# One chunk pipeline of a macaron block: one-hots at slot 1, z in slot 1 and silu in slot 3, and GpSimd's second product with C in slot 2

## The reference, cut to what matters

```
x = x + 0.5 * ffn(layernorm(x))            # f1
x = x + attn(layernorm(x))                 # p
x = x + 0.5 * ffn(layernorm(x))            # f2

ffn:  idx = argmax(softmax(x @ Wg + bg))                  # one of 8 experts per token
      out = gelu(x @ W1[idx] + b1[idx]) @ W2[idx] + b2[idx]
attn: xn = rmsnorm(x) * w;  x_path, z = split(xn @ Win.T)  # 256 channels each
      x_path = silu(causal conv of 4 taps(x_path) + conv_b)
      dt_x, B, C = split(x_path @ Wx.T)                    # 128, 16, 16
      dt = softplus(dt_x @ Wdt.T + dt_b)
      h = exp(dt * A) * h + (dt * x_path) * B              # along the tokens, 16 states per channel
      y = sum(h * C) + D * x_path
      out = (y * silu(z)) @ Wo.T + x
```

## Time and profile before

| | before |
|---|---|
| median of 3 runs | 1440.38 us (1437.05 to 1445.34) |
| the profiled execution, its own time | 1439.62 us |
| its span | 1437.8 us |
| TensorE busy | 1166.5 us (81%) |
| VectorE busy | 1061.8 us (74%) |
| GpSimd busy | 1066.9 us (74%) |
| ScalarE busy | 872.5 us (61%) |
| granted clock of TensorE, mean | 0.886 of 2.4 GHz |

### The profile page before, as it was taken

The page is one execution under the profiler, slowest core; times in us unless marked ns, Lnnn a source line. Parts: engine busy times, 40 slices in busy tenths (PEclk is TensorE's granted clock), DMA queues, the critical chain, the costliest instruction groups (busy, mean ns, idle before and its releaser), DMA issues.

```text
span 1437.8 us, 16300 instructions
## 1 busy us (share of the span) xinstructions
PE 1166.5 (81%) x5188; PEld 572.8 (40%) x5188; DVE 1061.8 (74%) x1713; ACT 872.5 (61%) x1171; POOL 1066.9 (74%) x900
## 2 busy tenths in 40 slices
PE   2678585879899988889888989888888887866777
PEld 1234232424444434344444444343444443423345
DVE  2021688888888797888888788978888888988910
ACT  0333746577667577676766675766767676574532
POOL 1023789888888797978888887979788888997600
PEclk9877697989899999899998999999999998878688
DMA  3002332323224051323233230503232323232000
GB/s 87 0 0 96 121 124 88 127 88 112 96 81 141 25 190 33 136 79 125 96 118 104 96 112 27 196 25 136 79 124 89 118 98 112 103 126 88 1 8 15
DMA packets 60406, 130.02 MB, mean 90 GB/s; under 512 B 7745, under 2 KB 26865, under 8 KB 52129
## 3 DMA queue, kind: packets, MB, share of 16 engines
q1 hardware_dynamic: 60320, 128.98, 26.1%
HBM read 106.94 MB, written 22.02 MB: 90 GB/s over the span
## 4 chain that ended last, share of the span: by engine, by line
PE 48%; DVE 24%; ACT 14%; POOL 6%; issue 6%; SPq 1%; DVEq 0%; ACTq 0%; DMA 0%; POOLq 0%
PE PY L479 12%; PE PH L464 11%; DVE dA L765 10%; PE G L453 9%; PE Y L491 6%; ACT hs L616 4%; DVE hb L769 4%; ACT dA L638 3%; PE PH L463 3%; DVE hb L763 3%; ACT hs L603 2%; POOL hb L943 2%; PE G L519 2%; ACT L616 2%; DVE stat L744 1%
## 5 line engine op out<-in xcount | busy, mean ns | idle before, releaser
L943 POOL TENSOR_TENSOR hb<-dtx_rep,bs 128x1024 f32<-128x1024 f32 x256 | 598.4, 2357 | 0.0
L765 DVE TENSOR_TENSOR_SCAN dA<-dA,hb 128x512 f32<-128x512 f32 x352 | 429.6, 1221 | 63.7 <-ACT dA L638 56.5
L638 ACT ACTIVATE dA<-dt_rep,A 128x512 f32<-128x512 f32 x512 | 341.0, 689 | 160.3 <-DVE hb L769 102.7
L464 PE MATMUL PH<-xnT,W 128*128 128x512 f32 x512 | 325.1, 720 | 0.0
L603 ACT COPY hs<-PH 128x512 f32<-128x512 f32 x256 | 149.2, 583 | 288.7 <-PE PH L464 288.5
L479 PE MATMUL PY<-W,hs 128*128 128x128 f32 x2048 | 294.7, 290 | 0.0
L479 PEld LDWEIGHTS PY<-W,hs 128*128 128x128 f32 x2048 | 259.8, 197 | 69.6 <-issue 60.0
L951 POOL TENSOR_TENSOR hb<-hb,cs 128x1024 f32<-128x1024 f32 x80 | 188.4, 2355 | 119.4 <-DVE hb L763 119.4
L769 DVE TENSOR_TENSOR hb<-dA,cs 128x512 f32<-128x512 f32 x352 | 243.5, 692 | 24.8 <-DVE dA L765 0.5
L763 DVE TENSOR_TENSOR_SCAN hb<-dA,hb 128x512 f32<-128x512 f32 x160 | 186.4, 1207 | 60.0 <-ACT dA L638 56.7
L491 PE MATMUL Y<-hb,Sel 128*32 128x512 f32 x1024 | 162.0, 707 | 30.9 <-POOL hb L951 23.7
(11 more groups left out here) (85 smaller groups left out, 1172.6 us busy)
## 6 DMA issues: line engine op xcount, KB each, us to landing
dtx_rep<-dtx_rows SPq DMA_DIRECT2D x32, 1024.0 KB, 6.4
dt_rep<-dt_rows SPq DMA_DIRECT2D x32, 1024.0 KB, 7.7
bs<-bc_rows SPq DMA_DIRECT2D x64, 256.0 KB, 3.6
cs<-bc_rows SPq DMA_DIRECT2D x64, 256.0 KB, 4.8
dtx_rows<-dtx SPq DMA_DIRECT2D x32, 256.0 KB, 2.5
dt_rows<-dt SPq DMA_DIRECT2D x32, 256.0 KB, 2.6
X<-in_x SPq DMA_DIRECT2D x16, 256.0 KB, 3.1
out<-X SPq DMA_DIRECT2D x16, 256.0 KB, 2.4
```

Source lines behind the costliest of these rows:

```text
L464: nc.tensor.matmul(PH[:, :], W1[:, e, :], xnT[:, w, :], start=False, stop=True).then_inc(ph_full, 1)
L638: nc.scalar.activation(dA[u % NA][:, :], dt_rep[:, h, g, :], ACT.Exp, scale=A[:, h, g, q:q + 1]).then_inc(decay, 1)
L765: nc.vector.tensor_tensor_scan(a, a, x_in_hb, 0.0, ALU.mult, ALU.add).then_inc(scan, 1)
L943: nc.gpsimd.tensor_tensor(hb[:, s % HR], dtx_rep[:, h, 2 * m:2 * m + 2, :], bs[:, q, None, :].broadcast_to([P, 2, CH]), ALU.mult).then_inc ...
```

## The change

Only the order of the work and one split between engines change.

- ln_f1 is transposed at the head of slot 0 (was slot 1), and ScalarE copies it to xnT between the two gelus of the iteration before (was behind slot 1).
- gate_f1 moves from slot 2 to the end of slot 0, its one-hot arithmetic on VectorE from ahead of slot 3 to ahead of slot 1. The transposes of the one-hots move from slot 5 to slot 6, behind the dt products, and their copy from ahead of slot 6 to ahead of slot 7.
- z0 and z1 move from slots 2 and 3 to slot 1. ScalarE's silu block moves from ahead of slot 4 to ahead of slot 3; the out product from slot 4 to slot 3, its add to behind slot 3, with the y add of f2 (was behind slot 2) ahead of it; bc, dt1 and dt0, their copies and softplus each one slot ahead.
- The statistics of f2 and GpSimd's root, norm, dt and dtx move one slot ahead. SyncE stores out and loads x in slot 5 (was 4), stores B and C in slot 5 (was 6) and the dt rows in slot 8 (was 9).
- GpSimd multiplies by C in slot 2, not in slot 3; VectorE does so in slot 3.
- A few units of the first and second products move within or by one slot.

```diff
-STAGES = [("ln_f1", 3, 0, 1, 0), ("gate_f1", 3, 1, 2, 1), ("z0", 1, 0, 2, 2), ("z1", 1, 1, 3, 1),
-          ("out", -1, 0, 4, 1), ("oh_f1", 3, 1, 5, 1), ("bc", 1, 0, 5, 0), ("dt1", 1, 1, 6, 0),
-          ("dt0", 1, 0, 6, 1), ("ln_f2", -1, 1, 9, 0), ("gate_f2", -1, 0, 10, 1), ("oh_f2", -1, 1, 12, 0),
+STAGES = [("ln_f1", 3, 0, 0, 0), ("gate_f1", 3, 1, 0, 2), ("z0", 1, 0, 1, 0), ("z1", 1, 1, 1, 2),
+          ("out", -1, 0, 3, 1), ("bc", 1, 0, 4, 1), ("dt1", 1, 1, 5, 0), ("dt0", 1, 0, 5, 1),
+          ("oh_f1", 3, 1, 6, 0), ("ln_f2", -1, 1, 9, 0), ("gate_f2", -1, 0, 10, 1), ("oh_f2", -1, 1, 12, 0),
           ("ln_p", 2, 0, 13, 0), ("x1", 2, 1, 14, 0), ("x0", 2, 0, 14, 1)]
-ACT_AT = {"ln_f1": 1.5, "silu": 4.0, "bc": 5.5, "dt1": 6.5, "dt0": 6.5, "soft": 7.0, "gelu_f2": 10.5,
-          "ln_f2": 9.5, "ln_p": 13.5, "taps": 14.0, "gelu_f1": 15.5}
-DVE_AT = {"gated1": 1.5, "y_f2": 2.5, "gate_f1": 3.0, "out": 4.5, "oh_f1": 6.0, "stats_f2": 5.0, "gated0": 9.5,
+ACT_AT = {"silu": 3.0, "bc": 4.5, "dt1": 5.5, "dt0": 5.5, "soft": 6.0, "gelu_f2": 10.5, "ln_f2": 9.5, "ln_p": 13.5,
+          "taps": 14.0, "gelu_f1": 15.5}
+DVE_AT = {"gate_f1": 1.0, "gated1": 1.5, "y_f2": 3.5, "out": 3.5, "stats_f2": 4.0, "oh_f1": 7.0, "gated0": 9.5,
           "y_f1": 10.0, "stats_p": 10.5, "gate_f2": 11.0, "stats_f1": 12.0, "oh_f2": 13.0, "tap01": 15.0, "tap2": 15.5}
-POOL_AT = {"root_f2": 6.5, "norm_f2": 7.0, "dt": 8.0, "dtx": 8.5, "root_p": 11.0, "norm_p": 12.0, "root_f1": 12.5,
+POOL_AT = {"root_f2": 5.5, "norm_f2": 6.0, "dt": 7.0, "dtx": 7.5, "root_p": 11.0, "norm_p": 12.0, "root_f1": 12.5,
            "norm_f1": 13.0}
-SP_AT = {"x_out": 4, "x_in": 4, "bc": 6, "b0": 8, "dt": 9, "b1": 10, "c0": 10, "b2": 12, "c1": 12, "b3": 14, "dtx1": 14,
+SP_AT = {"x_out": 5, "x_in": 5, "bc": 5, "b0": 8, "dt": 8, "b1": 10, "c0": 10, "b2": 12, "c1": 12, "b3": 14, "dtx1": 14,
          "c2": 14, "dt1": 15, "c3": 15}
-W1_AT = [[(8, 2, 8, 0, 3), (9, 2, 9, 0, 3), (10, 0, 10, 0, 3), (10, 2, 10, 3, 3),
+W1_AT = [[(8, 0, 8, 0, 3), (9, 0, 9, 0, 3), (10, 0, 10, 0, 3), (10, 2, 10, 3, 3),
...
-W2_AT = [[(s, 1, 2) for s in (5, 7, 7, 8, 8, 8, 9, 9)],
-         [(13, 1, -2), (14, 1, -2), (15, 1, -2), (15, 2, -2), (0, 1, -3), (0, 1, -3), (1, 1, -3), (1, 1, -3)]]
+W2_AT = [[(s, 1, 2) for s in (5, 6, 7, 7, 8, 8, 9, 9)],
+         [(13, 1, -2), (14, 1, -2), (15, 1, -2), (15, 2, -2), (0, 1, -3), (0, 1, -3), (1, 1, -3), (2, 1, -3)]]
...
-POOL_C = (1, 3, 5, 9, 14)
+POOL_C = (1, 2, 5, 9, 14)
...
                     if k == 0:
                         take_units(it, s, 3)
+                        if w == 0 and it.has(off + 1):
+                            copy_out(it.next(), "ln_f1", xnT[:, 0, :])
...
-                for w in range(2):
-                    if t == ACT_AT[f"ln_f{w + 1}"] and it.has(LN_OFF[w]):
-                        copy_out(it, f"ln_f{w + 1}", xnT[:, w, :])
+                if t == ACT_AT["ln_f2"] and it.has(-1):
+                    copy_out(it, "ln_f2", xnT[:, 1, :])
```

More of the change, by code:

```diff
@@ L172, in before, with next @@
         return Iteration(self.i0 - 1)
+    def next(self):
+        return Iteration(self.i0 + 1)
     def tiles(self, off, j=0, n=J):
```

## The result

The changed kernel takes 1375.68 us (median of 4 runs, 1373.46 to 1376.51) against 1440.31 (1437.05 to 1445.34): a ratio of 0.9546, 95% interval 0.9516 to 0.9576. The direction was right; the forecast of 1402 with its range down to 1383 was too slow by 26 us. The profiled execution has a span of 1374.2 us, 63.6 less than the 1437.8 of before.

The account below looks back on a forecast made before the run. VectorE's waits, partly behind TensorE's backlog, were taken as the bound. Eleven full iterations at 3.2 us (35), plus 8 for partial ones, 0 for fill and drain, less 5 for the clock, gave 38 off 1440.4: 1402, range 1383 to 1437.

Parts of the forecast that it names:

- What bounds it: Full iterations: VectorE idles 12.8 of 78.8 us, partly behind a TensorE backlog starting at its 2.50 us stall for bank 1.
- Slots 15 to 1: Iteration start: second gelu at 696.7, a 2.3 us wait for logits, slot 1 at 701.3, 1.4 us later than before.
- The out add: Slots 1 to 4: VectorE's add of the out product to X waits no more, 0.71 us won.
- Slots 4 to 10: TensorE runs without pause to 736.8; slot 10 starts at 737.5 instead of 740.61; 3.2 us taken per iteration.
- hidden, as said: GpSimd's moved work costs nothing, covered by its 2.5 us wait for the statistics of p.
- Swapped lengths, same sum: Slots 2 and 3: GpSimd's product moving to slot 2 swaps 2.34 and 3.85 us, leaving VectorE's sum unchanged.
- The allowance: 5 us taken off for slow-clock stretches of 4 us in TensorE's new unbroken run, in one of four iterations.
- Filling and draining: Pipeline start and end, some 200 us: no states to wait for, so gain 0, within 2 either way.
- Iterations 13 and 14: Partly run iterations: gain between nothing and 3.2 us each, taken as 2 each.
- The waits only move: Rival, chance 0.08: GpSimd's cover or unit 14's decay is 2 to 3 us worse; iteration stays 78.8, time 1436 to 1440.
- Gate ahead of slot 1: Slower rival, chance 0.09: late logits and transposes at iteration start lose some 1.4 us an iteration, time 1455.
- Better: Rival, chance 0.07: the two new waits (1.4 before unit 14, 1.3 at the y add) vanish too, 1.7 taken, time 1383.

Follow-up runs that it names:

- head_only: Kernel before with only the gate of f1 moved early (ln_f1, its copy between the gelus, gate product, one-hot arithmetic); 1475.0 us, ratio 1.0237.
- both_late: Changed kernel with the ln_f1 copy back behind the gelus and the first two W1 units of slots 8 and 9 back behind W2; 1433.1 us, ratio 0.9958.
- pool_extra: Changed kernel plus one unused GpSimd product in slot 5 of iterations 0 to 15; 1380.3 us, ratio 0.9573.
- pool_c3: Changed kernel with GpSimd's second product with C in slot 3 again, not slot 2; 1385.9 us, ratio 0.9607.
- each half alone: Kernel before with only the early gate of f1 (1475.0 us), or only the later moves from z1 and silu on, gate left in place (1450.5 us).
- copy_late: Changed kernel with the copy of ln_f1 to xnT back behind the second gelu and table load; 1412.9 us, ratio 0.9807.
- y_w2: Changed kernel with the y add of f1 behind slot 10 and the first W2 unit behind the one-hot transposes; 1365.2 us, ratio 0.9492.
- gate_first: Kernel y_w2 with, besides, the W1 unit of slot 0 behind the gate product; 1341.8 us, ratio 0.9332 of before.
- head_silu: Kernel head_only with z0 and z1 also moved to slot 1, silu and the out product to slot 3; 1407.4 us, ratio 0.9755.

## Why the prediction was right in sign and too small in size

**What bounds it: right.** VectorE's idle time was 12.8 us per iteration, and 3.4 of that went. The waits for ScalarE's decays behind TensorE's backlog are down to 0.5. That the backlog starts with z1's stall was only half of it: head_only has no such stall and all of the wait before slot 8. And the moved copy, which the walk had only as a cost of 0.58, carries the gain together with the W1 order (both_late, 78.43 per iteration without the two).

**Slots 15 to 1: right.** The walk's times are 31.0 us above those of the trace after. Timeline after, around the gate:

```profile
665.03 0.59 ACT L600 COPY xnT<-G 128x512 f32<-128x512 f32 x1
665.51 1.93 ACT L620 ACTIVATE hs<-hs 128x2048 f32<-128x2048 f32 x1
...
668.28 0.20 DVE L801 TENSOR_TENSOR G<-G,Bg 128x32 f32<-128x32 f32 x1 [1.90 <-PE G L543]
...
669.90 2.34 DVE L768 TENSOR_TENSOR_SCAN hb<-dA,hb 128x512 f32<-128x512 f32 x2 [0.21 <-DVE oh L812]
...
674.69 1.28 ACT L666 ACT_TABLE_LOAD   x1
...
676.73 3.27 PE L523 MATMUL G<-Wo,y 128*128 128x128 f32 x16 [2.14 <-ACT zs L666]
...
680.11 0.69 DVE L827 SCALAR_TENSOR_TENSOR X<-G,X 128x512 f32<-128x512 f32 x1 [0.67 <-PE G L523]
```

The second gelu was put at 696.7 (it is 665.5 + 31.0 = 696.5), slot 1 at 701.3 (700.9), silu at 706.3 (705.7). The wait for the logits is 1.9 where 2.3 stood.

**The out add: a miss of 0.7.** I gave the out product 1.8 us behind a pause of 1.8. TensorE stood 2.14 and then took 3.27, at a clock of 0.57 in the stretch of 677 to 681, 1.00 in those ahead and behind. So the add waits 0.67, nearly as before.

**Slots 4 to 10: right in sum, one place off.** Softplus ended at 693.1 + 31.0 = 724.1 (723.7 forecast). The 1.4 before unit 14 is 0.5, and 1.29 for the one-hots of TensorE stands beside it, which the walk had let pass. The y add waits 1.26 (1.3 forecast), and slot 10 starts at 706.68 + 31.0 = 737.7 (737.5).

```profile
693.27 0.41 DVE L823 COPY ohT<-G 24x512 bf16<-24x512 bf16 x1 [1.29 <-PE G L552]
...
694.19 1.23 DVE L770 TENSOR_TENSOR_SCAN dA<-dA,hb 128x512 f32<-128x512 f32 x1 [0.50 <-ACT dA L644]
...
706.07 0.69 DVE L827 SCALAR_TENSOR_TENSOR X<-PY,X 128x512 f32<-128x512 f32 x1 [1.26 <-PE PY L483]
```

**GpSimd: hidden, as said,** and pool_extra shows a cover of at least 1.9 us. "Swapped lengths, same sum" was wrong by 0.7 us of a short iteration (pool_c3). SyncE wasn't tested by itself; no wait for a DMA stands among VectorE's in the iteration shown.

**The clock: wrong, by 5 us.** The allowance was for a fall inside the new run. In the iteration shown the eleven stretches of 4 us from 661 to 705 read 1.00 but for the one at the out product, and from there to slot 10 (51 to 74 us behind the marker) the clock reads 0.97 to 1.00 in all of iterations 2 to 12. It falls in other places, at the out product and, in every second iteration, from 12 to 20 us behind the marker (0.50), which makes that iteration 1.5 us longer; the iterations of before have falls of their own and reach 80.5. The rule that I had set beside the row (the Trainium skill, TensorE: Matmul & The Clock Gate, "What's actually happening": activity releases the throttled state) gave 1397; for this run the trace agrees with it: the dense run kept the high level and the fall followed a pause.

**Filling and draining: this is the step that failed.** The term "Filling and draining, some 200 us, have no states to wait for [...] 0, within 2 either way" measured 17.75 us (13.65 in the fill beyond the 2 for iteration 0, 4.1 in the drain), of the 25.6 that were missing. It looked only at the one-hots. It should have walked the chain of the fill as the iteration was walked: the same moved copy that I costed there at 0.58 us of ScalarE takes a gelu and a table load out of a chain beside which nothing runs. Filling with iteration 0 gained 15.65 against 2 (both_late shows the whole of it to be the moved copy and the order of two W1 units, which the walk did not cost in the fill at all). Iteration 1 in turn gained nothing against 2. The drain gained 4.1 against 0; 3.0 of that is the out product of the last chunk. Before, TensorE makes four units of W1 between the last gating and it, after, three:

```profile
1369.68 0.69 DVE L828 TENSOR_TENSOR y<-Y,zs 128x512 f32<-128x512 f32 x1 [3.74 <-PE Y L491]
...
1380.31 1.95 PE L519 MATMUL G<-Wo,y 128*128 128x128 f32 x16
...
1382.36 0.69 DVE L822 SCALAR_TENSOR_TENSOR X<-G,X 128x512 f32<-128x512 f32 x1 [6.88 <-PE G L519]
```

```profile
1307.88 0.69 DVE L833 TENSOR_TENSOR y<-Y,zs 128x512 f32<-128x512 f32 x1 [2.66 <-PE Y L495]
...
1315.53 1.95 PE L523 MATMUL G<-Wo,y 128*128 128x128 f32 x16
...
1317.59 0.69 DVE L827 SCALAR_TENSOR_TENSOR X<-G,X 128x512 f32<-128x512 f32 x1 [2.53 <-PE G L523]
```

From gating to add that is 12.68 us before and 9.71 after.

**Iterations 13 and 14: mis-sized.** They gained 4.3 and 1.8 against 2 each. In 13 VectorE stood 4.91 us for a decay behind softplus, in a stretch that I had judged by its busy share alone; after, it stands 1.67. The 67.55 of iteration 14 after is the shortest of any kernel here (pool_extra, alike in the full iterations, has 71.01), so how much of its 1.8 is the change is open.

```profile
1203.08 1.23 DVE L765 TENSOR_TENSOR_SCAN dA<-dA,hb 128x512 f32<-128x512 f32 x1 [4.91 <-ACT dA L638]
```

```profile
1141.58 1.23 DVE L770 TENSOR_TENSOR_SCAN dA<-dA,hb 128x512 f32<-128x512 f32 x1 [1.67 <-ACT dA L644]
```

**The rivals.** "The waits only move" is what each half alone does, and worse: there, the new wait is longer than the old one. "Gate ahead of slot 1" has the right price mechanism: in copy_late and both_late VectorE waits some 4.3 and 4.1 us for the logits, and both_late has lost the gain of an iteration (78.43). In the kernel after they come soon enough. "Better" came nearest in its number (1383, measured 1375.7), but by luck: the two new waits did not vanish. y_w2, in which they do, gains 1.6 per iteration on the mean, near the 1.7 assumed, and the full 2.6 in its short iterations.

## What to carry to other kernels

Walk the fill and the drain of a software pipeline one instruction at a time, as its steady iteration: there most engines stand still, the chain is serial, and a copy that cost an iteration 0.6 us of ScalarE took 10.3 us out of the fill. Before a stall is called the root of a backlog, ask what else starts at the same place: removing z1's stall without the move of silu made the kernel 34.5 us slower, with it 33 us faster. When a walk ends with small waits left, each is worth an experiment; two of them, taken away by moves of a slot or less, and one unit of 1.4 us, gave 34 us more. And before a gain per iteration is put down to an edit, look at the iterations one by one: where the clock falls in some of them, the mean hid 0.7 us of one edit (pool_c3) and gave another 1.6 that its short iterations don't have (gate_first over y_w2).

## What was not expected of the hardware

A pause of TensorE can cost a second time, but need not. In a full queue the 16 products of the out product took 1.95. Behind 2.14 us without work they took 3.14 to 3.57 in the kernel after and up to 3.75 in head_silu, but 2.02 in five iterations of y_w2 and 2.4 to 3.5 in its others. Behind 1.67 us they took 2.02 in nine iterations of both_late and nine of gate_first in a row, and in copy_late 2.02 in five and 3.5 to 3.65 in five. Where the cost comes it is up to 1.8 us, nearly the pause itself. What decides whether it comes, the length of the pause alone doesn't tell, and no run here settles it.

The granted clock reads 1.00 from the start of every execution to its first fall, also where nothing has run yet. Up to 57 us two products of W1 took 2.08 us at that reading, as they did at 0.50 where an execution had its first fall early, and 1.12 later at 1.00: in the first tens of microseconds only the durations tell the level.
